# One pool of five PSUM banks for scores, row maxima and turned shifts, and blocks of four key tiles with a ring of twenty, in a two-layer attention and feed-forward kernel

## What is computed

```python
qkv = einsum('bsd,ed->bse', x, w_qkv) + b_qkv            # split into q, k, v of 16 heads
scores = einsum('bhqd,bhkd->bhqk', q, k) / sqrt(32) + causal
attn = softmax(scores, axis=-1)
out = einsum('bhqk,bhkd->bhqd', attn, v)                  # heads joined again
x = layernorm(x + einsum('bsd,ed->bse', out, w_out) + b_out)
hidden = relu(einsum('bsd,hd->bsh', x, sign(up_weight)) * up_scale)
x = layernorm(x + einsum('bsh,dh->bsd', hidden, sign(down_weight)) * down_scale * output_scale)
```

## Time and profile before

| what | value |
|---|---|
| median of three runs | 790.63 us (789.76 to 791.11) |
| the profiled execution: device time, its span | 792.56 us, 790.8 us |
| busy, share of the span: PE | 745.9 us, 94% |
| PEld; DVE; ACT; POOL | 502.7 us, 64%; 451.8 us, 57%; 323.9 us, 41%; 356.2 us, 45% |
| mean granted TensorE clock | 0.98 |

### The profile page before, as it was taken

One profiled execution on the slowest core, in us unless ns is written; L12 is line 12 of the kernel. 1 busy time (PEld: TensorE's weight loads), 2 busy tenths in 40 slices (PEclk: granted clock), 3 DMA queues, 4 the chain that ended last, 5 costly groups with the idle time before them and its releaser, 6 DMA issues.

```text
span 790.8 us, 11678 instructions
## 1 busy us (share of the span) xinstructions
PE 745.9 (94%) x4032; PEld 502.7 (64%) x4032; DVE 451.8 (57%) x1086; ACT 323.9 (41%) x631; POOL 356.2 (45%) x487
## 2 busy tenths in 40 slices
PE   6899999999999999999999898999999999999994
PEld 4687555654656556565544453688778787878882
DVE  4176495785867858668565562533286329433514
ACT  5211365555555555456545556523232223221210
POOL 4451466384673945739332411442344234323333
PEclk9999999999999999999989899999999999999998
DMA  6966364434545256352467240503002001000101
GB/s 226 316 176 173 96 175 123 136 96 133 169 126 143 82 148 164 105 148 81 134 200 259 95 161 8 174 27 121 14 27 97 24 15 40 15 1 0 54 1 53
DMA packets 44619, 85.71 MB, mean 108 GB/s; under 512 B 4880, under 2 KB 13584, under 8 KB 44432
## 3 DMA queue, kind: packets, MB, share of 16 engines
q1 hardware_dynamic: 35536, 79.72, 33.6%
q10 hardware_dynamic: 9024, 5.24, 2.3%
HBM read 55.33 MB, written 29.36 MB: 107 GB/s over the span
## 4 chain that ended last, share of the span: by engine, by line
PE 74%; DVE 15%; issue 3%; ACT 3%; DMA 3%; POOL 1%; SPq 0%; ACTq 0%; DVEq 0%; POOLq 0%
PE ps_heads L1020 9%; PE ps_unit L953 8%; PE ps_score L990 7%; PE ps_proj L913 7%; PE ps_proj L1063 7%; PE ps_score L1080 6%; PE ps_unit L1036 6%; PE ps_sum L1014 5%; PE ps_unit L1063 5%; DVE maxes L790 4%; DVE heads_sb L812 4%; PE ps_heads L1080 3%; PE ps_sum L1080 3%; PE ps_sum L933 1%; PE ps_score L933 1%
## 5 line engine op out<-in xcount | busy, mean ns | idle before, releaser
L688 ACT ACTIVATE probs<-ps_score 128x512 f32<-128x512 f32 (+3 forms) x360 | 171.7, 492 | 173.7 <-PE ps_score L990 166.5
L632 POOL TENSOR_TENSOR hid_low<-hid_raw,hid_high 128x512 fp32r<-128x512 f32 x64 | 85.1, 1330 | 174.5 <-DVE hid_high L863 171.4
L786 DVE CUSTOM_DVE_ANT_0 ps_unit<-ps_unit,causal 128x128 f32<-128x128 f32 (+3 forms) x256 | 122.0, 511 | 67.9 <-PE ps_unit L953 66.4
L953 PE MATMUL ps_unit<-stack 96*128 96x512 f32 (+3 forms) x384 | 136.6, 371 | 9.9 <-DVE maxes L786 4.7
L990 PE MATMUL ps_score<-stack 98*128 98x512 f32 (+2 forms) x360 | 136.7, 386 | 4.1 <-ACT probs L688 2.3
L596 POOL TENSOR_SCALAR_AFFINE_SELECT probs<-probs 128x128 f32<-128x128 f32 x256 | 74.3, 297 | 139.5 <-ACT probs L688 134.8
L953 PEld LDWEIGHTS ps_unit<-stack 96*128 96x128 f32 x384 | 72.2, 191 | 57.7 <-DVE maxes L790 23.4
L863 DVE CAST hid_high<-hid_raw 128x512 fp32r<-128x512 f32 x64 | 27.1, 425 | 126.6 <-ACT hid_raw L743 126.3
L990 PEld LDWEIGHTS ps_score<-stack 98*128 98x128 f32 x360 | 68.4, 191 | 46.4 <-ACT probs L688 32.1
L790 DVE TENSOR_REDUCE maxes<-ps_unit 128x1 f32<-128x512 f32 x128 | 79.3, 685 | 21.3 <-PE ps_unit L953 21.2
L1020 PE MATMUL ps_heads<-probs,v_rows 128*32 128x512 f32 (+3 forms) x768 | 82.6, 508 | 5.9 <-DVE heads_sb L814 5.9
(11 more groups left out here) (185 smaller groups left out, 1224.4 us busy)
## 6 DMA issues: line engine op xcount, KB each, us to landing
stack<-qk_parts SPq DMA_DIRECT2D x96, 256.0 KB, 4.7
qk_parts<-parts SPq DMA_DIRECT2D x32, 512.0 KB, 2.9
v_all<-h_even ACTq DMA_DIRECT2D x16, 256.0 KB, 3.5
v_rows<-v_all SPq DMA_DIRECT2D x8, 512.0 KB, 4.2
heads_t<-heads_sb SPq DMA_DIRECT2D x16, 256.0 KB, 3.2
raw<-up_w SPq DMA_DIRECT2D x8, 512.0 KB, 3.6
x_tile<-x_rows SPq DMA_DIRECT2D x16, 256.0 KB, 4.7
raw<-down_w SPq DMA_DIRECT2D x8, 512.0 KB, 3.7
```

Source lines behind the costliest of these rows:

```text
L632: nc.gpsimd.tensor_tensor(hid[1][:, (HM * s + n) % 3, :], hid_raw[:, n % 2, :], hid[0][:, (HM * s + n) % 3, :].bitcast(FP32), ALU.subtract ...
L688: nc.scalar.activation(probs[:, (NP * s + n) % RING, 0:width], score_bank(s, n)[:, off:off + width], ACT.Exp, scale=SCALE).then_inc(s_exp, 1)
L786: nc.vector.tensor_tensor_reduce(ps_unit[n % 3][:, 0:width], ps_unit[n % 3][:, 0:width], causal[:, HALF - width:], 1.0, NEG, ALU.add, ALU.max,
L953: nc.tensor.matmul(ps_unit[n % 3][:, 0:width], stack[s % 2][0:96, 1, f, h, i % 4 * P:(i % 4 + 1) * P], stack[s % 2][0:96, 0, c, h, 0:width ...
```

## The change

Scores, maxima and turned shifts of steps 0 to 6 no longer have banks of their own. A new function hands out five banks in turn, each time the one unused for longest, and every user waits for the reader of the bank's last user. Blocks of steps 0 to 5 are four key tiles, at slots 19.6, 36 and 52, and `probs` has 20 tiles. `sum_added` goes to slot 51.9. `MAXIMA` and `BLOCK` get other slots. A smaller scratch area for DMA descriptors makes room for the six tiles.

```diff
-RING = 14
+RING = 20
-PAIRED = [13, 13, 19.6, 19.6, 28, 28, 36, 36, 44, 44, 52, 52]
+FOURS = [19.6] * 4 + [36] * 4 + [52] * 4
-MAXIMA = ([11.5 + 0.5 * u for u in range(3)] + [13.4 + 0.48 * u for u in range(13)]
-          + [26.3 + 0.6 * u for u in range(3)] + [28.4 + 0.53 * u for u in range(14)] + [37.5 + 0.66 * u for u in range(15)])
-BLOCK = [(1, 2, 0.5, 0.98, 13.05, 15.8, 18.5), (1, 3, 13.3, 0.5, 19.65, 22.4, 24.8),
-         (2, 0, 20.5, 1.2, 34.4, 37.2, 40), (2, 1, 36.3, 0.6, 44.05, 46.8, 49.2)]
+MAXIMA = [10.8 + 0.55 * u for u in range(16)] + [25.8 + 0.62 * u for u in range(16)] + [36.8 + 0.62 * u for u in range(16)]
+BLOCK = [(1, 2, 0.5, 0.85, 10.4, 13.2, 15.7), (1, 3, 11.2, 0.7, 19.65, 22.4, 24.8),
+         (2, 0, 21.5, 1.15, 36.05, 38.8, 41.3), (2, 1, 38.3, 0.8, 47.7, 50.5, 53)]
...
-            put(t + 43.9, "sum_added", s)
+            put(t + 51.9, "sum_added", s)
...
+def share(todo):
+    order, had, users = [3, 4, 5, 0, 1, 2], {}, {}
+    for what, s, n in todo:
+        if what not in ("score", "max", "shift"):
+            continue
+        if what == "score":
+            may = (2, 3, 4, 5) if s == STEPS - 1 else (0, 1, 2, 3, 4)
+        else:
+            may = (0, 1, 2, 3, 4) if s else (0, 1, 2)
+        bank = next(k for k in order if k in may)
+        users[what, s, n] = bank, had.get(bank)
+        had[bank] = what, s, n
+        order.remove(bank)
+        order.append(bank)
+    return users, had
...
-                    wait(pe, s_max, NU * s + n - 2)
+                    bank_read(users[what, s, n][1])
...
-                    if s < STEPS - 1 or n < 2:
-                        wait(pe, s_exp, NP * s + n - 1)
-                    elif n > 3:
-                        pe.wait_ge(s_exp, NP * s + n - 3)
+                    bank_read(users[what, s, n][1])
...
-                        if n == 14:
+                        if n == 15:
                             act.wait_ge(s_pv, NP * STEPS)
                             act.wait_ge(s_st[1], 16 * STEPS)
```

More of the change, by code:

```diff
@@ L142, in plan @@
             put(t + n, "score", s, n)
-        paired = s < STEPS - 2
-        for g, at in enumerate(PAIRED if paired else ALONE[s % 2]):
+        fours = s < STEPS - 2
+        for g, at in enumerate(FOURS if fours else ALONE[s % 2]):
             put(t + at, "pv", s, g)
@@ L407, in heads_in, with bank @@
             return heads_raw if s else h1_even
-        def score_bank(s, n):
-            return (ps_score + [ps_proj, ps_unit[2]])[n % 4] if s == STEPS - 1 else ps_score[n % 2]
+        def bank(what, s, n):
+            return (ps_unit + ps_score + [ps_proj])[users[what, s, n][0]]
         def hidden_used(eng, steps):
@@ L672, in _ @@
                     act.wait_ge(s_mt, 2 * s + n + 1)
-                    nc.scalar.activation(shift_h[:, :], ps_turn[n][0:NU0, 0:P], ACT.Copy,
+                    nc.scalar.activation(shift_h[:, :], bank(what, s, n)[0:NU0, 0:P], ACT.Copy,
                                          scale=-1.0).then_inc(s_mh, 1)
@@ L684, in _ @@
                     wait(act, s_pv, NP * s + n - RING + 1)
-                    k = n - RING - GH * FIRST_ADD
-                    if s < ADDING and 0 <= k < GH * (LAST_ADD - FIRST_ADD):
-                        act.wait_ge(s_add, NA * s + (k if k < GH else k - GH) + 1)
-                    nc.scalar.activation(probs[:, (NP * s + n) % RING, 0:width], score_bank(s, n)[:, off:off + width],
+                    s0, k = (NP * s + n - RING) // NP, (n - RING) % NP - GH * FIRST_ADD
+                    if 0 <= s0 < ADDING and 0 <= k < GH * (LAST_ADD - FIRST_ADD):
+                        act.wait_ge(s_add, NA * s0 + (k if k < GH else k - GH) + 1)
+                    nc.scalar.activation(probs[:, (NP * s + n) % RING, 0:width], bank(what, s, n)[:, off:off + width],
                                          ACT.Exp, scale=SCALE).then_inc(s_exp, 1)
@@ L785, in _ @@
                         width = P * (i % 4 + 1)
-                        nc.vector.tensor_tensor_reduce(ps_unit[n % 3][:, 0:width], ps_unit[n % 3][:, 0:width],
+                        nc.vector.tensor_tensor_reduce(bank(what, s, n)[:, 0:width], bank(what, s, n)[:, 0:width],
                                                        causal[:, HALF - width:], 1.0, NEG, ALU.add, ALU.max,
@@ L789, in _ @@
                     else:
-                        nc.vector.tensor_reduce(maxes[:, 1, col:col + 1], ps_unit[n % 3][:, :], AXIS_X,
+                        nc.vector.tensor_reduce(maxes[:, 1, col:col + 1], bank(what, s, n)[:, :], AXIS_X,
                                                 ALU.max).then_inc(s_max, 1)
@@ L799, in _ @@
                     dve.wait_ge(s_mh, 2 * s + n + 1)
-                    nc.vector.scalar_tensor_tensor(out=shift_l[:, :], in0=ps_turn[n][0:NU0, 0:P], scalar=-1.0,
+                    nc.vector.scalar_tensor_tensor(out=shift_l[:, :], in0=bank(what, s, n)[0:NU0, 0:P], scalar=-1.0,
                                                    in1=shift_h[:, :].bitcast(FP32), op0=ALU.mult,
@@ L894, in _, with bank_read @@
         def _(pe):
+            def bank_read(user):
+                if user is None:
+                    return
+                what, s, n = user
+                if what == "score":
+                    pe.wait_ge(s_exp, NP * s + n + 1)
+                if what == "max":
+                    pe.wait_ge(s_max, NU * s + n + 1)
+                if what == "shift":
+                    pe.wait_ge(s_ml, 2 * s + n + 1)
             for what, s, n in todo:
@@ L946, in _ @@
                         pe.wait_ge(s_stack[2 * f + 1], 48 * (s + 1))
-                    if n == 2:
-                        wait(pe, s_ml, 2 * s)
-                    if n == NU1:
-                        pe.wait_ge(s_ml, 2 * s + 1)
-                    wait(pe, s_max, NU * s + n - 2)
-                    nc.tensor.matmul(ps_unit[n % 3][:, 0:width], stack[s % 2][0:96, 1, f, h, i % 4 * P:(i % 4 + 1) * P],
+                    bank_read(users[what, s, n][1])
+                    nc.tensor.matmul(bank(what, s, n)[:, 0:width], stack[s % 2][0:96, 1, f, h, i % 4 * P:(i % 4 + 1) * P],
                                      stack[s % 2][0:96, 0, c, h, 0:width], start=True, stop=True).then_inc(s_unit, 1)
@@ L979, in _ @@
                         pe.wait_ge(s_md[1], 32 * (s + 1))
-                    if s == STEPS - 1 and n == 2:
+                    if s == STEPS - 1 and users[what, s, n][0] == 5:
                         pe.wait_ge(s_qk, NB * STEPS)
-                    if s == STEPS - 1 and n == 3:
-                        pe.wait_ge(s_ml, 2 * STEPS)
-                    if s < STEPS - 1 or n < 2:
-                        wait(pe, s_exp, NP * s + n - 1)
-                    elif n > 3:
-                        pe.wait_ge(s_exp, NP * s + n - 3)
-                    nc.tensor.matmul(score_bank(s, n)[:, 0:width + off],
+                    bank_read(users[what, s, n][1])
+                    nc.tensor.matmul(bank(what, s, n)[:, 0:width + off],
                                      stack[s % 2][0:98, 0, j // 4, h, j % 4 * P:(j % 4 + 1) * P],
```

23 lines of the change are left out of this document (10 added, 13 removed).

## The result

The changed kernel takes 795.41 us, the median of six runs (794.2 to 799.8), beside 790.69 us for the kernel before in the same comparison: a ratio of 1.0066, 95% interval 1.0036 to 1.0095. It is slower by 0.7%. The forecast was 796.4 us with 0.60 on slower, so the time and the sign came out as predicted. The profiled execution took 795.16 us, its span is 793.4 us against 790.8 us.

The account below looks back on a forecast made before the run. PE was taken as the bound, busy 745.9 of 790.8 us. 6 × 0.33 + 6 × 0.45 + 5 × 0.97 − 2.8 − 1.0 = +5.75 us gave a 796.55 us span, median 796.4; 8 in 10 runs from 780 to 806.

Parts of the forecast that it names:

- part 3: After the block at 36 to slot 4: PE waits at two projection starts; +0.97 us, bounds +0.4 to +1.3.
- part 2: Slot 20 to the end of the block at 36: block work moves behind DVE's chain; +0.45 us, bounds +0.2 to +0.9.
- The idle times that I named as signs: PE idle ahead of first projection matmuls: about 2 us in part 1, 1.2 after block 36, 1.3 near slot 48.
- part 1: Slot 4 to the end of the block at 19.6: eviction wait replaces norm wait; +0.33 us, bounds 0 to +0.6.
- rival 2: Projection starts: evictions are covered, PE does not wait there, some −16 us in all, 774 us; chance 0.05.
- rival 3: Part 1's new 2 us wait: the clock falls once a step, 10.2 us on top, 806.6 us; chance 0.10.
- Step 5: End of step 5, no projection following: second wait absent, 14.9 us against 17.66 before, −2.8 us once.
- Steps 6 and 7: In step 6, shared banks and wider slots may take a third of 2.8 us waits for DVE: −1.0 us.
- Start-up: Up to the first score of step 0: the start-up order changes nothing, 0 us.
- Rival 1: Every step: the banks pay, all 21 late loads go, 12.6 us off the sum, 783.9 us; chance 0.20.

Follow-up runs that it names:

- own_fours: Kernel before with its own score and maxima banks, but the new order (blocks of four, new tables) and the ring of twenty: 799.43 us.
- shared_pairs: Changed kernel with the old order put back (blocks of two, old tables, sum_added at 43.9), keeping shared banks and ring of twenty: 780.66 us.
- combined: Changed kernel with two key tiles back at slot 28, first, third and fourth evictions earlier, first and fourth projections' matmuls closer together: 789.60 us.
- shared_later: shared_pairs with the blocks at 13 and 28 moved to 14.1 and 28.9 and the second projection started and spaced to match: 789.12 us.

## Why the prediction was right, and where it was not

**The sign and the mechanism.** I forecast that the waits for evictions take the place of what the pool saves, and that blocks moved behind DVE's chain are paid in full. Both are there: 0.31 and 1.13 us behind L687 in part 3, the block of part 2 at 13.87 us. own_fours and shared_pairs separate the two halves of the change as the argument did. The idle times that I named as signs came out smaller, except the one near slot 48 (1.13 for 1.3 us): in part 1 PE is idle for 0.33 us behind L687 and 0.83 us behind the load, where I had 2 us behind L687, and after the block at 36 for 0.31 us behind L687 and 0.21 us behind DVE's shift_l, where I had 1.2. In the second place PE had 0.7 us of work by columns in the 1.83 us, so it lost 1.1 us by starts, while the rows count idle time only from the end of the matmul before. Steps are 1.45 us farther apart than before, not 1.75.

**Part 1, +0.33 predicted, −0.16 measured.** The mis-sized term is the time of the exponentials: 2.83 us instead of 3.15. It lies in the four of 384 columns: I took 0.494 us each, the mean duration of rows 6, but they overlap and start 0.41 us apart, 1.65 us instead of 1.98. The three smaller ones came out at 1.18 us for 1.17 with a wait of 0.20 us for PE among them, which is luck. PE restarts 0.06 us behind the eviction instead of 0.1, and the remainder is 7.09 us instead of 7.15. A gain of 0.16 us lies just below my lower bound of 0. What I named as the cause of the part's end was incomplete as well: combined showed that DVE's norm and sixteen maxima hold the block at 11.6 us even when the eviction is early. I had that chain in rival 2, ending at 10.9 us, 0.7 us too early.

**Part 2, +0.45 predicted, +0.28 without a clock fall, +0.7 over the six.** The start of the block was right to 0.03 us. The block itself is 3.57 us and not 3.70: a merged block saves a boundary, which I had deducted in part 1 and forgotten here. The clock falls are rival 3's mechanism at another place: three of six steps, 2.6 us of the total, where I had expected them, if at all, in part 1 at 2 us of waiting, and counted against them that this wait is shorter than 2.26 us and lies in dense work. In own_fours one came in part 1, behind 1.02 us. The Trainium skill ("TensorE: Matmul & The Clock Gate", HAM oscillation — how this bites in real kernels) warns of idle gaps between bursts of matmuls that are longer than this one. Here a gap of 1.36 us in dense work was followed by a fall in three steps and by none in three others.

**Part 3, +0.97 predicted, +1.33 measured.** The restarts of the two projections came out within 0.2 us (1.83 for 2.0, 10.10 for 9.96). Mis-sized are the work between them, 6.51 us from the fourth projection's first to its last matmul instead of 6.16, which its early start half hides, and the end: seven matmuls to sum_added 1.83 us instead of 1.65 (the first after a wait starts 0.33 us ahead of the next). Five times this difference is 1.8 us. It is the largest error against me and the order's largest price: part 3 carries 2.1 of the 3.05 us.

**Step 5** came out at 15.24 us against 14.9 predicted, with the clock at 1.00 between the steps. **Steps 6 and 7** gave 3.4 us instead of 1.0, for a reason that I did not have: one fall of 6.8 us in place of two. The term itself had the wrong sign: the shared banks were to take a third of the waits for DVE, and brought a new wait of 3.79 us and a cost of 0.6 to 1.6 us at equal low clock. **Start-up**: −1.95 us by one execution's clock, where I had nothing.

**The sum** was therefore right in part by errors that cancel: steps 0 to 5 are 8.0 us longer instead of 6.7, and start-up and the last two steps give back 5.4 instead of 1.0. Without start-up, the falls in part 2, and steps 6 and 7, the measured terms are 6 × (−0.16 + 0.28) + 5 × 1.33 − 2.4 = +5.0 us; that the medians differ by 4.7 us does not confirm this sum, since their executions have such falls in them and the −2.4 holds the fall that is gone between steps 5 and 6.

**Rival 1 was half right.** Pooled banks do pay, 1.6 us a step or some 10 us in all, once the order leaves DVE its cover: nearly the 12.6 us of all late loads. I gave it 0.20 as a statement on the whole change; its error was not the price but the condition. The rule of the Trainium skill ("Perfetto Trace Analysis", Optimizing Tensor Performance, Matmuls) on rotating banks, which the prediction weighs, is borne out by the pool with the old order (−1.6 us a step, −0.52 us of it in part 2) and does not hold in part 2 of the new order (+0.37 us with the pool).

**Open**: what decides whether the clock falls after the 1.36 us wait. Times of combined spread over 8 us and those of shared_later over 13 us with the same program, with the lower mean clock in the slower executions; in the profiled ones six and five steps had a fall. shared_pairs had no fall in steps 0 to 5 of its two profiled executions and spreads over 4 to 5.5 us, about as the kernel before does. Open too are what 1.2 of the order's 3.05 us a step go to, and why the new order has fewer falls in steps 6 and 7.
